# An LSTM's recurrent products on TensorE: widths of 32 columns against 48 and 4, and h's two halves stored apart

## The reference, cut to what matters

```python
x = x + _L0_cond_ref(x, cond_1024, Wx, Wh, b)          # (2, 1024, 256)
x = x + _L1_cond_ref(x, cond_1024, ...)                # mixture of experts on every token

# _L0_cond_ref: h0 = cond_1024, c0 = 0, for each of 1024 time steps
a = xw_t + prev_h @ Wh                                 # (2, 1024)
i, f, o, g = sigmoid(a_i), sigmoid(a_f), sigmoid(a_o), tanh(a_g)
next_c = f * prev_c + i * g
next_h = o * tanh(next_c)
```

## Time and profile before

| | us |
|---|---|
| median of 3 runs | 2023.9 (2023.49 to 2024.84) |
| the profiled execution's own time | 2023.38 |
| its span, first to last instruction | 2021.6 |
| TensorE matmuls busy | 1655.5 (82%) |
| VectorE busy | 1619.1 (80%) |
| ScalarE busy | 806.0 (40%) |
| GpSimd busy | 135.1 (7%) |

### The profile page before, as it was taken

One profiled execution on the slowest core, in us unless ns is written; L12 is line 12 of the kernel. 1 busy time (PEld: TensorE's weight loads), 2 busy tenths in 40 slices (PEclk: granted clock), 3 DMA queues, 4 the chain that ended last, 5 costly groups with the idle time before them and its releaser, 6 DMA issues. The chain is left out here.

```text
span 2021.6 us, 95636 instructions
## 1 busy us (share of the span) xinstructions
PE 1655.5 (82%) x37356; PEld 1456.2 (72%) x37356; DVE 1619.1 (80%) x14263; ACT 806.0 (40%) x5529; POOL 135.1 (7%) x457
## 2 busy tenths in 40 slices
PE   7888888788888888888888887888888888888888
PEld 6777777777777777777777776777777777777777
DVE  6888788787878878788787877878788787887874
ACT  3554343343433434343343433434334343433432
POOL 0000000000000000000000000000000000000000
PEclk9999999999999999999999999999999999999999
DMA  5000000000000000000000000000000000000000
GB/s 232 3 3 3 3 6 3 6 3 3 6 3 6 3 3 6 3 6 3 6 3 3 6 3 6 3 3 6 3 5 3 4 4 3 6 3 6 3 3 7
DMA packets 7223, 19.85 MB, mean 10 GB/s; under 512 B 1136, under 2 KB 5616, under 8 KB 5872
## 3 DMA queue, kind: packets, MB, share of 16 engines
q1 hardware_dynamic: 6768, 13.73, 1.8%
HBM read 11.63 MB, written 2.10 MB: 7 GB/s over the span
## 5 line engine op out<-in xcount | busy, mean ns | idle before, releaser
L687 PE MATMUL gates<-hh,wh_lo 128*128 128x32 f16 x16384 | 820.7, 194 | 349.1 <-DVE hh L608 346.1
L687 PEld LDWEIGHTS gates<-hh,wh_lo 128*128 128x128 f16 x16384 | 597.9, 98 | 544.5 <-DVE hh L608 541.2
L695 PE MATMUL gates<-hh,wh_hi 128*128 128x32 f16 x16384 | 696.7, 183 | 4.2 <-DVE hh L620 4.2
L578 DVE TENSOR_TENSOR_SCAN gates<-part_fac,gates 128x12 f32<-128x12 f32 x3072 | 395.6, 186 | 262.3 <-PE gates L695 238.7
L330 ACT ACTIVATE gates<-gates 128x4 f32<-128x4 f32 x1024 | 161.8, 158 | 1051.5 <-DVE gates L578 1051.5
L695 PEld LDWEIGHTS gates<-hh,wh_hi 128*128 128x128 f16 x16384 | 572.9, 96 | 6.1 <-DVE hh L620 6.1
L340 ACT ACTIVATE to<-o_sum 128x4 f32<-128x4 f32 x1024 | 212.3, 207 | 116.0 <-DVE o_sum L578 0.8
L605 DVE TENSOR_SCALAR to<-to 128x4 f32<-128x4 f32 x1024 | 175.0, 171 | 71.3
L597 DVE TENSOR_TENSOR_SCAN gates<-gates,addend 128x12 f32<-128x12 f32 x1024 | 194.9, 190 | 0.0
L591 DVE SCALAR_TENSOR_TENSOR addend<-gates,c_now 128x4 f32<-128x4 f32 x1024 | 167.7, 164 | 25.1
L333 ACT ACTIVATE addend<-gates 128x8 f32<-128x8 f32 x1024 | 182.2, 178 | 0.0
(11 more groups left out here) (131 smaller groups left out, 1571.3 us busy)
## 6 DMA issues: line engine op xcount, KB each, us to landing
rw_sb<-rw SPq DMA_DIRECT2D x2, 2048.0 KB, 22.2
sw_sb<-sw SPq DMA_DIRECT2D x3, 1024.0 KB, 13.3
outT<-osb SPq DMA_DIRECT2D x16, 128.0 KB, 2.2
x_sb<-xT SPq DMA_DIRECT2D x1, 1920.0 KB, 9.7
wh_sb<-wh SPq DMA_DIRECT2D x1, 1024.0 KB, 4.7
wx_sb<-wx SPq DMA_DIRECT2D x1, 1024.0 KB, 6.5
x_sb<-xT SPq DMA_DIRECT2D x1, 128.0 KB, 4.8
eye_sb<-eye SPq DMA_DIRECT2D x1, 64.0 KB, 6.0
```

What stands on the lines that cost most here:

```text
L578: return v.tensor_tensor_scan(dst, part_fac[:].rearrange("p c j -> p (c j)"), parts[q], 0.0, ALU.mult, ALU.add)
L687: mm(copies(q, m, n)[:, :, :, 0:1], wh_lo[:, c, (q * KC + m) * P:(q * KC + m + 1) * P], again(hh[:, c, :, 1:2], n), start=(m == 0 and c == ...
L695: last = mm(copies(q, m, n)[:, :, :, 0:2], wh_hi[:, c, (q * KC + m) * P:(q * KC + m + 1) * P], again(hh[:, c, :, :], n), start=False, stop ...
```

## The change

WIDE becomes 48. Low products of all gates, and the high ones of G and O, move 48 columns (24 and 12 copies); the high ones of F and I move 4 (one copy). h is stored as (chunk, half, batch) instead of (chunk, batch, half), so that the two batches of one half are neighbours; a high product therefore writes its columns in the order j, b instead of b, j. The scratch columns in the gates' banks move up from 256 to 384, and o's sum moves from SBUF to F's bank. VectorE copies only G's and I's seeds before h_hi; F's seeds come behind h, then h_lo, c_now, O's seeds. TensorE does low(G), low(I), waits for F's seeds, does low(F), and waits for O's seeds before low(O). The splitting of x leaves GpSimd: ScalarE makes the high part behind step 60, VectorE the low one in two halves behind steps 61 and 63.

```diff
-WIDE = 32
+WIDE = 48
 APART = 16
+BESIDE = 384
-SPLIT_AT = 5
+SPLIT_HI, SPLIT_LO = 60, (61, 63)
-        hh = sb("hh", [P, KC, B, 2], F16)
-        h_lo, h_hi = hh[:, :, :, 0], hh[:, :, :, 1]
+        hh = sb("hh", [P, KC, 2, B], F16)
+        h_lo, h_hi = hh[:, :, 0, :], hh[:, :, 1, :]
-        o_sum = sb("o_sum", [P, HC * PARTS])
+        tf, o_sum = beside(F, HC, BESIDE + 32), beside(F, HC * PARTS, BESIDE + 64)
...
             def low(q):
-                        mm(copies(q, m, n)[:, :, :, 0:1], wh_lo[:, c, (q * KC + m) * P:(q * KC + m + 1) * P],
-                           again(hh[:, c, :, 1:2], n), start=(m == 0 and c == 0), stop=False, skip_group_check=True)
+                        mm(copies(q, m, n)[:, :, :, 0], wh_lo[:, c, (q * KC + m) * P:(q * KC + m + 1) * P],
+                           hh[:, c, 1:2, :].broadcast_to([P, n, B]), start=(m == 0 and c == 0), stop=False, skip_group_check=True)
-            def high(q):
-                n = WIDE // B // 2
+            def high(q, n):
-                        last = mm(copies(q, m, n)[:, :, :, 0:2], wh_hi[:, c, (q * KC + m) * P:(q * KC + m + 1) * P],
-                                  again(hh[:, c, :, :], n), start=False, stop=True, skip_group_check=True)
+                        last = mm(copies(q, m, n).rearrange("p r b j -> p r j b")[:, :, 0:2, :],
+                                  wh_hi[:, c, (q * KC + m) * P:(q * KC + m + 1) * P],
+                                  hh[:, c, :, :].rearrange("p (r j) b -> p r j b", r=1).broadcast_to([P, n, 2, B]),
+                                  start=False, stop=True, skip_group_check=True)
...
-            def lstm(s):
+            def lstm(s, tile):
                 pe.wait_ge(s_hhi, s + 1)
-                low(F)
                 low(G)
                 low(I)
+                if s:
+                    pe.wait_ge(s_seeded, 2 * s - 1)
+                elif tile:
+                    pe.wait_ge(s_seeded, 2 * TS - 1)
+                low(F)
                 pe.wait_ge(s_hlo, s + 1)
-                high(F).then_inc(s_mul, 1)
-                high(G).then_inc(s_mul, 1)
-                high(I).then_inc(s_mul, 1)
+                high(F, 1).then_inc(s_mul, 1)
+                high(G, WIDE // B // 2).then_inc(s_mul, 1)
+                high(I, 1).then_inc(s_mul, 1)
+                if s:
+                    pe.wait_ge(s_seeded, 2 * s)
+                elif tile:
+                    take_back(pe, s_seeded, 2 * TS)
                 low(O)
-                high(O).then_inc(s_mul, 1)
+                high(O, WIDE // B // 2).then_inc(s_mul, 1)
...
# VectorE, in lstm(s)
-                v.tensor_copy(gif_xw, of_gif(seeds[:, piece % 2, at, 0:O * HC]))
+                v.tensor_copy(gi_xw, of_gi(seeds[:, piece % 2, at, 0:F * HC]))
...
                 v.tensor_tensor(h_now, to1[:], tc, ALU.mult).then_inc(s_own, 1)
+                v.tensor_copy(f_xw, seeds[:, piece % 2, at, F * HC:O * HC]).then_inc(s_seeded, 1)
+                dve.wait_ge(s_own, 2 * s + 2)
+                v.scalar_tensor_tensor(h_lo, h_hi, -LO, by_batch(h_now), ALU.mult, ALU.add).then_inc(s_hlo, 1)
                 ins = v.tensor_scalar(c_now[:], cs[:, :, 2], 0.5, None, ALU.mult)
...
-                v.tensor_copy(o_xw, seeds[:, piece % 2, at, O * HC:GATES])
-                dve.wait_ge(s_own, 2 * s + 2)
-                v.scalar_tensor_tensor(h_lo, h_hi, -LO, by_batch(h_now), ALU.mult, ALU.add).then_inc(s_hlo, 1)
+                v.tensor_copy(o_xw, seeds[:, piece % 2, at, O * HC:GATES]).then_inc(s_seeded, 1)
...
# ScalarE, behind step SPLIT_HI
+                activation(x_part[0][:], x_sb[:, :, (tile + 2) * TT:(tile + 3) * TT], ACT.Identity, scale=s_xin).then_inc(s_parts, 1)
# VectorE, behind steps SPLIT_LO
+                ins = v.scalar_tensor_tensor(x_part[1][:, k, :], x_sb[:, k, (tile + 2) * TT:(tile + 3) * TT], s_xin,
+                                             x_part[0][:, k, :], ALU.mult, ALU.subtract)
# GpSimd
-                g.tensor_tensor(x_scaled[:], x_sb[:, :, at], s_xin..., ALU.mult).then_inc(s_parts, 1)
-                g.tensor_copy(x_part[0][:], x_scaled[:]).then_inc(s_parts, 1)
-                g.tensor_tensor(x_part[1][:], x_scaled[:], x_part[0][:], ALU.subtract).then_inc(s_xpart, 1)
```

More of the change, by code:

```diff
@@ L96, in cond_resid_kernel, with beside @@
         parts = [gates[:, q * BANK:q * BANK + HC * PARTS] for q in range(4)]
-        gif_xw = gates.rearrange("p (q n) -> p q n", n=BANK)[:, G:O, 0:HC * PARTS].rearrange(
+        gi_xw = gates.rearrange("p (q n) -> p q n", n=BANK)[:, G:F, 0:HC * PARTS].rearrange(
             "p q (c j) -> p q c j", j=PARTS)[:, :, :, PARTS - 1]
-        o_xw = parts[O].rearrange("p (c j) -> p c j", j=PARTS)[:, :, PARTS - 1]
-        def beside(q, n, at=256):
+        f_xw, o_xw = (parts[q].rearrange("p (c j) -> p c j", j=PARTS)[:, :, PARTS - 1] for q in (F, O))
+        def beside(q, n, at=BESIDE):
             return gates[:, q * BANK + at:q * BANK + at + n]
         g_sum, i_sum, f_sum = (beside(q, HC * PARTS) for q in (G, I, F))
-        fac = beside(I, HC * 3, 288).rearrange("p (c j) -> p c j", j=3)
-        tf = beside(F, HC, 288)
+        fac = beside(I, HC * 3, BESIDE + 32).rearrange("p (c j) -> p c j", j=3)
+        tf, o_sum = beside(F, HC, BESIDE + 32), beside(F, HC * PARTS, BESIDE + 64)
         cs = beside(O, HC * 3).rearrange("p (c j) -> p c j", j=3)
-        tc = beside(O, HC, 288)
+        tc = beside(O, HC, BESIDE + 32)
         xw_first = [xw_next[:, 0:TT], up_rt[:, 0:TT]]
@@ L191, in cond_resid_kernel @@
         s_xmax, s_wxs = sem("x_looked_over"), sem("wx_scale_ready")
-        s_parts, s_xpart = sem("next_x_scaled"), sem("next_x_in_parts")
+        s_parts, s_xpart = sem("next_x_hi_ready"), sem("next_x_in_parts")
         s_link, s_own = sem("vector_setup_step"), sem("vector_step_done")
@@ L199, in cond_resid_kernel @@
         s_mul, s_sum, s_tanh = sem("f_g_i_o_multiplied"), sem("f_g_i_o_c_summed"), sem("f_o_c_tanh")
-        s_scan = sem("scan_operands_ready")
+        s_scan, s_seeded = sem("scan_operands_ready"), sem("f_o_seeds_in_place")
         s_piece, s_staged, s_added = sem("piece_of_steps_done"), sem("piece_staged"), sem("h_added_to_x")
@@ L260, in _ @@
             stage(0, slice(GATES, (HS + 1) * GATES))
[L262 to L266, removed]
-                g.tensor_copy(x_part[0][:], x_scaled[:]).then_inc(s_parts, 1)
-                take_back(pool, s_parts, 2)
-                g.tensor_tensor(x_part[1][:], x_scaled[:], x_part[0][:], ALU.subtract).then_inc(s_xpart, 1)
             def piece(q, tile):
@@ L299, in _ @@
                     g.partition_all_reduce(wtop[:, 1:3], wmax[:, 1:3], P, RMAX).then_inc(s_top, 1)
-                if q == SPLIT_AT:
-                    split(slice(2 * TT, 3 * TT))
             finish()
@@ L306, in _ @@
                     piece(q, it)
-                    if q == SPLIT_AT:
-                        split(slice((it + 2) * TT, (it + 3) * TT))
                 finish()
@@ L339, in lstm @@
                 act.wait_ge(s_sum, 5 * s + O_OF)
-                activation(to[:], last_of(o_sum[:]), ACT.Tanh, scale=0.5).then_inc(s_tanh, 1)
+                activation(to[:], last_of(o_sum), ACT.Tanh, scale=0.5).then_inc(s_tanh, 1)
                 act.wait_ge(s_sum, 5 * s + C_OF)
@@ L375, in mixture, with split_hi @@
                     activation(ge[:], up_rt[:, 0:RC * TT].rearrange("p (c t) -> p c t", c=RC), ACT.Gelu).then_inc(s_act, 1)
+            def split_hi(tile):
+                activation(x_part[0][:], x_sb[:, :, (tile + 2) * TT:(tile + 3) * TT], ACT.Identity, scale=s_xin).then_inc(s_parts, 1)
             for s in range(TS):
@@ L379, in _ @@
                 first_tile(s)
+                if s == SPLIT_HI:
+                    split_hi(0)
             take_back(act, s_sum, 5 * TS)
@@ L386, in _ @@
                     mixture(s, xw_at)
+                    if s == SPLIT_HI and it < NT - 1:
+                        split_hi(it)
                 take_back(act, s_sum, 5 * TS)
@@ L397, in _, with of_gi @@
             done = [0]
-            def of_gif(columns):
+            def of_gi(columns):
                 return columns.rearrange("p (q c) -> p q c", c=HC)
@@ L471, in _ @@
             dve.wait_ge(s_xwc0, MC + 1)
-            v.tensor_copy(gif_xw, of_gif(xw[:, 0:O * HC]))
+            v.tensor_copy(gi_xw, of_gi(xw[:, 0:F * HC]))
+            v.tensor_copy(f_xw, xw[:, F * HC:O * HC])
             v.tensor_copy(o_xw, xw[:, O * HC:GATES]).then_inc(s_hhi, 1)
@@ L592, in lstm @@
                 dve.wait_ge(s_mul, 4 * s + O_OF)
-                summed(o_sum[:], O).then_inc(s_sum, 1)
+                summed(o_sum, O).then_inc(s_sum, 1)
                 dve.wait_ge(s_scan, 3 * s + 3)
@@ L653, in first_tile, with split_lo @@
                                            wx_slice(wx_part[0], i, 2 * NW), ALU.mult, ALU.subtract).then_inc(s_lo, 1)
+            def split_lo(k, tile):
+                dve.wait_ge(s_parts, tile + 1)
```

(14 more changed lines are left out.)

1 line of the change is left out of this document (removed).

## The result

| | before | after |
|---|---|---|
| median, us | 2024.4 (2023.5 to 2025.3, 4 runs) | 2262.0 (2259.7 to 2262.7, 4 runs) |
| span of the profiled execution | 2021.6 | 2259.9 |
| ratio | | 1.117, 95% interval 1.115 to 1.119 |

What follows compares the result with a forecast made beforehand. The kernel was taken as a chain of 1024 time steps; +246 ns per step x 1023 = +252 us, less 7 us, takes the 2021.6 us span to 2266, so 2268 us forecast. Range: 2058 to 2290.

Steps and rivals of the forecast that it cites:

- The working price: TensorE's PSUM writes: neighbours written together only from an even place, so low products pay 2 column times per column, high 1.5.
- points 1, 2: Per step: twelve low products at 48 columns, +160 ns; G's high products at 48 in order j, b, +69.
- point 3: High products of F and I at four columns: starts stay 25 ns apart, I's last ends sooner, -17 ns.
- point 4: O's products take 340 ns after I's last instead of 218, delaying o's sum and the cell's scan: +34 ns.
- points 5 to 8: h_lo sooner, TensorE's new seed waits, VectorE's extra copy and later work, o's sum in PSUM: 0 each, the last +- 5.
- point 9: x's split off GpSimd: h_lo no longer slowed, -0.45 us 16 times, -7.2 us; 0 in the new places.
- the source as the price: Interleaving of h's halves causes both surcharges, so low products fall to the 25 ns floor: 1973 us; chance 0.16.
- the run rule: Every break of a written run costs one column time, wherever it lies: 2069 us; chance half of 0.20.
- a price per copy: Every copy in a product costs two column times; low 42.5 ns, G 32.5: 2193 us; chance half of 0.20.
- the cost of the form: Products cost by instruction form: low stay at 29 ns, high at 25, whatever they move: 2009 us; chance 0.03.
- that rival: F's and I's narrow products let TensorE's clock fall: 0.5 us a step, decisive from one step in ten; chance 0.03.

Runs made afterwards that it cites:

- the pair that differs by one address: Changed kernel with copies side by side, low products writing neighbouring pairs from even places, then the same shifted one column to odd places: 1962.1 and 2165.7 us.
- the first experiment: Kernel before with h's halves stored apart and nothing else: 2019.2 us, ratio 0.9977.

## Why the prediction was right, point by point

Medians over the steps of both kernels, in ns from h_hi's start, good to 1 ns; the prediction's terms beside them:

| | before | after | change | predicted |
|---|---|---|---|---|
| first low product | 219 | 208 | -11 | 0 |
| from there to f's sum | 659 | 802 | +143 | +160 (twelve low), F's narrow end -17 |
| f's sum to g's | 100 | 190 | +90 | +69 + 17 |
| g's sum to i's | 100 | 95 | -5 | -17 |
| i's sum to the cell's scan | 411 | 440 | +29 | +34 |
| scan to the next h_hi | 414 | 409 | -5 | 0 |
| step | 1903 | 2144 | +241 | +246 |

- *The working price* (points 1, 2) held to the nanosecond: 42.5 ns for low products and G's and O's high ones. It was read from the stretch at the lower clock and from the first product behind a wait, and the pair that differs by one address shows it by itself. The first product behind the wait, which nothing holds up, bears it out once more: it lasts 203 ns in before, 216 in after and 197 with the copies side by side, as 64, 96 and 48 column times would have it.
- *The narrow ends* (point 3) were right for F. For I the sum came 5 earlier and not 17, held by the scan ahead of it. Where i's tanh ends the wait, the shorter scan gives the rest back, 14 in all in the kernel before; in after it gives nothing, since there O's products end the wait.
- *O's products* (point 4): 29 against 34. The scan followed 95 ns behind o's sum, inside the range given.
- *h_lo, the waits for seeds, the longer list of VectorE, o's sum in PSUM* (points 5 to 8): no wait shows any of them. h_lo starts 318 ns behind h_hi and not about 300, but nothing hung on it. What the prediction left out is the 11 ns by which the first low product follows sooner. It is the length of h_hi's write, whose median was 161 ns in before and is 150 in after:
```profile
L601 DVE SCALAR_TENSOR_TENSOR hh<-to,gates x1024: 144/150/159, 24.2 to 2220.4; 128x4 f16<-128x4 f32 x171
```
  In every kernel here the first low product starts 57 or 58 ns behind the end of that write. With the halves apart alone the write is 4 ns shorter; what takes the other 7 off it was not tested.
- *The split* (point 9): -7.2 predicted, -7 measured alone (0.9966 x 2024.5), nothing in the new places. With the copies side by side the last two steps of a tile are 29 and 38 ns longer than the others; whether that is the split was not tested.
- The sum: 241 x 1023 = 246.5 us for the step; 7.6 fewer from steps 48 and 49; 2.5 fewer from steps that were long before with the clock at half speed or for the router, and 2 more ahead of the first step and behind the last: 238 us, the difference of the spans. That the step came within 5 ns is partly luck: the misses were +12 (I's sum) and +4 (G's) against -11 (the first product), -5 (O's products) and -5 (the last row). Two of the recorded sums are off by a microsecond, without effect: 2009 should be 2010, and the range's lower end 2059.

The rivals: the source as the price fell with the first experiment, the run rule with the pair, a price per copy with both, the cost of the form with the low gap of 42.5. The clock did not fall in after (0.997 to 0.999 in its four executions, with TensorE's matmuls busy for 88% of the span). With the copies side by side the narrow products did cost clock, as that rival had it: 59 to 86 us at half speed, under one step in twenty, not one in ten.

## What to carry to other kernels

Count a matmul's writes, not only its columns: two column times for each even-aligned pair of neighbouring fp32 columns when both are written in a row, two for every column by itself, and 25 ns at least from start to start here. The order counts too: the places 0, 1, 3, 4 cost 1.5 column times per column, 0, 3, 1, 4 cost 2. If copies are only there to fill, lay them side by side from an even place, and let the reader step over them: the same 48 columns cost 42.5 ns apart and 25 side by side, some 300 us of this kernel. To see a price that a floor hides, look for a stretch at the lower clock, or for the first product behind a wait.

## What was not expected of the hardware

- High products of F and I narrowed from 32 to 4 columns left the gaps as they were and took the clock to half speed for 24 to 60 us in five executions, instead of 8 to 16, so that what was gained at TensorE was partly lost there. In the changed kernel at `WIDE = 32`, which has the same widths but, among other things, another order of G's and O's columns, it was 12 to 16 us in ten executions. What decides was not found.
- VectorE's sums of 12 columns, where the first of them waits for TensorE, follow each other after 95 or 96 ns at the least in nearly all steps (76 to 90, and a few times 42, in steps in which the products had long ended), and one that follows after 95 or 96 lasts 172 to 175 ns instead of 187.
- Sums that read every 24th column of PSUM (f's lasts 187 ns, as with neighbouring columns), and a source that repeats one element 24 times in a row (gaps of 25 ns), cost nothing that shows.
- GpSimd's x_lo, which reads SBUF and writes fp16, held up h_lo by 0.45 us in each of 16 tiles. VectorE's two instructions ahead of it (c_now and O's seeds) ran beside x_lo too and kept their 152 to 157 ns each time; they read one operand, and h_lo reads two from SBUF. GpSimd's fp32 copies and sums of 32 to 128 columns ran beside h_lo some 250 times and left it at 151 to 158 ns, but each of them had started after h_lo, and x_lo 0.09 us before it. So the type, the two operands and who comes first are not told apart.
